# One constant: how many indirect DMAs GpSimd keeps in flight, 3 where it was 2

## The reference: what is computed

```python
xn = layernorm(x)
s  = channel_attention(xn, Wq, Wk, Wv, Wo)        # 256 x 256 scores per sequence, softmax over channels
g  = silu(moe(xn))                                # 32 experts, 8 groups
out = x + s * g

# moe: each row picks 3 of 8 groups by their best score, then 6 experts among those
y = sum over the 6 experts e of weight_e * (silu(xn @ w1[e].T) * (xn @ w3[e].T)) @ w2[e].T
y = y + shared_expert(xn)
```

## Time and profile before

| what | value |
|---|---|
| median of 3 runs | 969.05 us (965.66 to 969.32) |
| the profiled execution, its own time | 964.12 us |
| its span in the trace | 962.4 us |
| TensorE busy | 596.8 us (62%), granted clock 0.804 on average |
| VectorE busy | 506.7 us (53%) |
| GpSimd busy | 399.2 us (41%), 384 indirect DMAs |
| DMA traffic | 174.75 MB, 182 GB/s over the span |

### The profile page before, as it was taken

The page is one execution under the profiler, slowest core; times in us unless marked ns, Lnnn a source line. Parts: engine busy times, 40 slices in busy tenths (PEclk is TensorE's granted clock), DMA queues, the critical chain, the costliest instruction groups (busy, mean ns, idle before and its releaser), DMA issues.

```text
span 962.4 us, 13698 instructions
## 1 busy us (share of the span) xinstructions
PE 596.8 (62%) x3728; PEld 486.4 (51%) x3728; DVE 506.7 (53%) x1412; ACT 341.5 (35%) x684; POOL 399.2 (41%) x401
## 2 busy tenths in 40 slices
PE   5788782928375776001979776758486765658540
PEld 4567551817164654001968665546375654547430
DVE  7877863736374771000535555546465645646543
ACT  3343431332323242001646443435254443435330
POOL 0135345455364663663001444343444444453443
PEclk9798795867768686655979797879799897979875
DMA  9994572634524223224437675758677675848552
GB/s 335 390 356 164 182 262 93 234 132 140 210 73 141 76 93 132 82 82 136 145 120 218 192 237 171 219 154 251 176 220 224 189 208 168 241 148 259 164 170 76
DMA packets 134232, 174.75 MB, mean 182 GB/s; under 512 B 12433, under 2 KB 120722, under 8 KB 133266
## 3 DMA queue, kind: packets, MB, share of 16 engines
q1 hardware_dynamic: 109698, 107.77, 34.3%
q0 software_dynamic: 18432, 50.36, 17.4%
q10 hardware_dynamic: 6032, 15.76, 4.7%
HBM read 81.56 MB, written 92.28 MB: 181 GB/s over the span
## 4 chain that ended last, share of the span: by engine, by line
DMA 57%; issue 21%; POOL 9%; PE 8%; DVE 4%; POOLq 1%; ACT 0%; SPq 0%; DVEq 0%; ACTq 0%
DMA early<-slots_d,slot_at 30%; DMA slots_d<-early,slot_at 23%; POOL slots_d L391 7%; PE ps L696 4%; DMA slots_d<-pad 3%; DVE ps L957 3%; POOL early L408 2%; PE ps L715 2%; PE ps L684 1%; PE ps L706 1%; DVE work L974 1%; POOLq L391 0%; SPq L290 0%; DMA work<-slots_d 0%; DMA slots_d<-early 0%
## 5 line engine op out<-in xcount | busy, mean ns | idle before, releaser
L408 POOL DMA_INDIRECT early<-slots_d,slot_at x192 | 191.7, 999 | 316.9 <-DVE ps L957 108.2
L391 POOL DMA_INDIRECT slots_d<-early,slot_at x192 | 205.4, 1070 | 237.8 <-DMA slots_d<-early,slot_at 170.5
L696 PE MATMUL ps<-w_all,work 128*128 x1344 | 186.5, 294 | 57.3 <-issue 54.2
L696 PEld LDWEIGHTS ps<-w_all,work 128*128 128x128 f16 x1344 | 140.5, 105 | 83.1 <-issue 60.4
L684 PE MATMUL ps<-ident,work 128*128 128x128 f32 x448 | 75.2, 294 | 140.1 <-DMA work<-slots_d 65.9
L957 DVE SCALAR_TENSOR_TENSOR ps<-early,wk,ps 128x256 f32<-128x256 f32 x160 | 77.8, 486 | 116.9 <-DMA early<-slots_d,slot_at 115.5
L684 PEld LDWEIGHTS ps<-ident,work 128*128 128x128 f32 x448 | 54.7, 151 | 155.7 <-issue 81.4
L974 DVE SCALAR_TENSOR_TENSOR work<-ps,work 128x512 f16<-128x512 f32 x112 | 76.8, 686 | 103.6 <-ACT work L517 102.1
L517 ACT ACTIVATE work<-ps 128x512 f16<-128x512 f32 x112 | 66.6, 595 | 141.0 <-PE ps L684 128.1
L715 PE MATMUL ps<-w_all,work 128*128 x672 | 99.9, 289 | 2.5 <-DVE work L987 2.0
L524 ACT ACTIVATE work<-ps 128x256 f32<-128x256 f32 x112 | 43.0, 384 | 157.1 <-PE ps L696 127.4
(11 more groups left out here) (140 smaller groups left out, 811.6 us busy)
## 6 DMA issues: line engine op xcount, KB each, us to landing
work<-slots_d SPq DMA_DIRECT2D x112, 256.0 KB
slots_d<-early SPq DMA_DIRECT2D x112, 256.0 KB
slots_d<-pad SPq DMA_DIRECT2D x7, 3072.0 KB, 15.5
w_all<-in_wexp ACTq DMA_DIRECT2D x7, 1536.0 KB, 6.9
slots_d<-pad SPq DMA_DIRECT2D x1, 7168.0 KB, 30.0
s_all<-in_x SPq DMA_DIRECT2D x8, 512.0 KB, 4.8
ysh_d<-work ACTq DMA_DIRECT2D x8, 512.0 KB
early<-ysh_d SPq DMA_DIRECT2D x32, 128.0 KB
```

What stands on the lines that cost most here:

```text
L391: pool.indirect_dma_start(slots_d[:, :], bass.IndirectOffsetOnAxis(ap=slot_at[:, at:at + 1], axis=0), xn[b % XN_RING][:, t, :], None, boun ...
L408: pool.indirect_dma_start(gath[:, at % RING, :], None, slots_d[:, :], bass.IndirectOffsetOnAxis(ap=slot_at[:, at:at + 1], axis=0), bounds_ ...
L696: mm = pe.matmul(ps[:, 2 + p % 2, h * 2 * I:(h + 1) * 2 * I], xT[p % 2][:, x_low, h, k, :], w16[:, bass.ds(at_weights[2 * p + h] + w_low * ...
```

## The change

The constant is 3 instead of 2:

```diff
 XN_RING = 3
-FLIGHT = 2
+FLIGHT = 3
 BATCH_ROWS = TB * TOP_K
```

## The result

The changed kernel takes 856.75 us (median of 4 runs, 849.25 to 861.13) against 967.99 us before (965.66 to 969.32; also four runs, of which the table ahead of the prediction had three). The ratio is 0.885, with a 95% interval of 0.878 to 0.891. The forecast was 821 us. The profiled execution took 858.25 us, with a span of 856.5 us.

What follows compares the result with a forecast made beforehand. It took the count of indirect DMAs in flight to bound both phases: 962.4 us less 75 (scatters), 57 (gathers) and 12 (tail), plus 1.7 around the span, gives 820.1, named as 821 us; range 785 to 865.

Steps and rivals of the forecast that it cites:

- The count in flight was the limit of both phases: Scatters and gathers: POOL, allowed two in flight, waits for landings; 108.2 us put down to DVE line 957 belong to this.
- full ring: Gathers: the reading, rejected by the prediction, that 108.2 us of POOL's waiting come from all 12 buffers being in use.
- term of 75 us: All 192 scatters: 67 in slow stretches of 166 us, 125 others in 168 us, sum 334, so 75 us saved.
- `normal` stops waiting for scatters: Phase 1, DVE line 755: waits for scatters, such as 16.8 us before `normal(4)`, go or nearly go.
- Twelve pairs take 45.5 us: Phase 2: 12 us around a `hold` plus 34 us at a DMA share of 0.95, about 45.5 us instead of 53.6.
- signs of being wrong: Landings half as long again, POOL's DMA_INDIRECT over 1.0 us, PE waiting for `slots_d`, or similar waits for ring or stores.
- sum for the seven stretches: Phase 2, seven stretches of twelve pairs: 318.5 us instead of 375.4, so 57 us saved.
- The tail: End of phase 2, from 916.50 us with 19 gathers left: end at about 950, 12 us saved, between 8 and 16.
- the gathers gain nothing since the DMA engines are full: Rival, phase 2: the DMA engines bound the gathers, so no gain there; 877 us, 868 with a small gain; chance 0.14.
- both floors are reached: Rival: PE's own pace reached in phase 2, DVE's chain nearly in phase 1; 777 us, 795 with one; chance 0.16.
- It does nothing: Rival: POOL's own issue is already the limit, or the queue works on two at a time; 964 us; chance 0.04.
- slower since loads come late: Rival, phase 2: gathers crowd out loads of pairs (line 330) and PE waits for rows; 971 us; chance 0.02.

Runs made afterwards that it cites:

- e2: Changed kernel with only the gathers at three in flight, the scatters at two as before: 890.57 us, ratio 0.923 to the kernel before.
- e9: The changed kernel without any edit, run again on another chip, the same as for e8: 824.28 us, ratio 0.850 to the kernel before.
- e1: Changed kernel with only the scatters at three in flight, the gathers at two as before: 888.14 us, ratio 0.921 to the kernel before.
- e4: Changed kernel with four in flight for both scatters and gathers instead of three: 771.06 us, ratio 0.796 to 0.803 around 0.799.
- group 2: The runs e5, e6 and e7, made on one chip beside the kernel before: 857.99, 857.35 and 897.99 us, against 969.47 us before.
- e3: Changed kernel, three in flight, with POOL waiting for a small memset of its own after each indirect DMA: 921.56 us, ratio 0.956.
- e7: Changed kernel with six in flight for both scatters and gathers instead of three: 897.99 us, ratio 0.928 to the kernel before.
- e10: The kernel of e4 (four in flight for both) without any edit, on the same chip as e11: 775.72 us, ratio 0.799.
- e11: The kernel of e7 (six in flight for both) without any edit, on another chip: 760.92 us, ratio 0.783 to the kernel before.
- e8: The kernel of e4 (four in flight for both) without any edit, on the same chip as e9: 771.50 us, ratio 0.796.
- e5: The changed kernel itself, run once more without any edit: 857.99 us, ratio 0.882 to the kernel before.
- e6: Changed kernel plus one semaphore that nobody uses, which shifts the numbers of those made after it: 857.35 us, ratio 0.884.

## Why the prediction was right, and where its sizes were off

**The count in flight was the limit of both phases.** Right. The prediction read the 108.2 us that the profile put down to DVE's line 957 as waiting for landings, and e2 shows that the gathers alone, with a third in flight, are worth 73 us. The 71.6 us that the profile puts down to this line after the change are again no full ring, and only in part landings. I took the last 180 gathers and, for each wait over 0.4 us, the latest of its conditions. Before, all 145 such waits (215 us) end with a landing. In e9 66 do (78 us), and 8 others, of 50 us, end with the landing of a pair's **store**, up to 7.5 us each, one for each `hold` after which PE's pairs come late. In the result it is 68 us for landings and 89 for stores, if a store lands 3.2 us after its issue as in the earlier trace rows. With four in flight it is 23 us for landings and 81 for stores, with six 0.5 and 98. So a limit that bound no gather before is the next one. The prediction had it only among its signs of being wrong. Gather 60 of e9, where the profile again names DVE, and the store it needed; that store landed at 572.36, while the sum that frees the buffer had ended 10.9 us before the gather's start:

```profile
564.81 0.99 POOL L408 DMA_INDIRECT early<-slots_d,slot_at  x1 [0.30 <-issue]
573.25 0.99 POOL L408 DMA_INDIRECT early<-slots_d,slot_at  x1 [7.45 <-DVE ps L957]
...
568.53 0.36 SPq L334 DMA_DIRECT2D slots_d<-early  x1
```

**A scatter costs 1.28 us in quiet, and three go in a slow landing's time.** Right, as the rows of POOL above show. Counted as in the prediction (a landing over 3 us makes a slow place), the result has 65 scatters in slow stretches of 165.5 us, forecast 67 in 166. The other 127 take 1.43 us each, forecast 1.34. So of the term of 75 us, e9 has 68.4 and e1 73.4 us. That a third is worth nothing in quiet is refuted by e1's gain and the spacing of 1.28 for 1.59 us. The 3.17 us of the prediction have two parts. In e2's quiet scatters, two in flight as before, the last of the 16 landing increments comes 2.41 us after the issue starts, and the scatter that waits for it starts 0.76 us later. The 2.3 us that the prediction estimated by the Trainium skill (DMA: Bandwidth & Descriptors, section "Anatomy of one DMA — SWDGE (gpsimd) path") agree with the 2.41. What the conclusion drawn from them left out is the 0.76 us that POOL needs to start again. In the result itself it was 62.1 us, and the missing part is the late increments: DVE's `slot_at` of sequences 2 to 6 came 38.4 to 40.0 us apart, instead of the 37.6 of a chain that doesn't wait, and that of sequence 7 after 81.8 us, at 341.6, where e9 has it at 306.1.

**`normal` stops waiting for scatters.** Nearly. The wait of 16.8 us before `normal(4)` is gone, line 755 follows line 748 at once:

```profile
146.33 0.16 DVE L748 TENSOR_TENSOR rstd<-rough,newt 128x4 f32<-128x4 f32 x1
146.56 1.38 DVE L755 TENSOR_SCALAR early<-s_all,mv,rstd 128x256 f32<-128x256 f32 x4
```

In e9 two such waits are left, of 15.5 us together. The last scatter was forecast at 370; it is issued at 382.95 after, at 376.65 in e9.

**Twelve pairs take 45.5 us.** Right in e9 (317.2 / 7 = 45.3) and e2 (45.2), 49.4 in the result. Its working was less good than its outcome, and that the two agree is in part luck: it took the DMA engines as the limit, at a share of 0.95 outside the `hold`, and forecast a share above 0.8. The share is 0.78 to 0.79. Its sum slips too: 12 + 34 is 46 us, which is 53 us saved and not 57. With four and six in flight the same stretches fall only to 43.0 and 43.4 us at 0.81, as this window of e4 shows:

```profile
436.10:737.40 301.30, 243.36 (x2019) 210.48 (x2017) 209.24 (x475) 156.60 (x364) 166.29 (x166) 0.90 0.81 253
```

So three in flight still cost 2 us per 12 pairs in the count itself. With four and six, most of what the gathers still wait is for stores (above); what sets the 43 us was not taken apart. That a third gather lengthens the others' landings could be seen to be small: the mean from a gather's issue to the end of its last packet is 3.24 us before, 3.43 after and 3.53 in e9.

**The step that was mis-sized.** It is the sum for the seven stretches, with 57 us forecast and 29.5 measured in the result. The prediction let every wait of ACT and DVE for PE last as long as before. In e9, where they did, the term is 58.2 us (375.4 to 317.2). In the result 45 evictions started late by 65.6 us. The stage table splits the 33.3 us by which the result's span exceeds e9's, for one and the same program: 6.3 us up to the first load, 28.8 in the seven stretches, 0.3 between, and 2.1 the other way in the tail. No step of the prediction had a place for this, and the trace before gave no cause to look: 4 late starts of 448.

**The tail.** Forecast 12, measured 14.2 and 12.1. The last gather starts 8.7 us before the end, as before.

**The rivals.** That the gathers gain nothing since the DMA engines are full fell with e2. That both floors are reached fell too: with three in flight neither was, and with six some 38 us per sequence, against 37.6 for DVE's own chain, and 43.4 us per 12 pairs, against 41.8, came near. "It does nothing" and "slower since loads come late" did not occur. There was one rival missing, on the slow side: that PE's increments come late while POOL issues without a pause. It took 33 us here, and didn't change the sign. The range held the result (856.75 against 865), but its upper part had been made for gathers that gain little, which is not what happened: that it held is luck.

**What stays open.** Why increments of PE arrive late in the result and in group 2, and not in the three other groups, is not settled. In the runs that have it, most late starts stand where POOL issues without a pause; in the runs that don't, such issuing does nothing. Whether it is the chip or what went on on it at the time, these runs can't tell; each chip was met once, and the result's own is not known. Nor can they tell whether the delay would be there without the profiler's recording, whose records are incomplete just where it occurs. Whether four in flight would suffer, and whether the pause of e3 would protect, was not measured where it occurs. Since the pause costs some 100 us (921.56 for e3, 824.28 for e9), it would not be worth it there either: even e7, at 898, is faster than e3.

**The best version** is four or six in flight. Six is best where nothing comes late (760.9 us, ratio 0.783) and worse than three where it does (898 against 858). Four gave 771 to 776 us on three chips, but wasn't run where something comes late, so which number is safer is open. From four to six, e10 to e11 on one chip, it is 14.8 us: the first load moves from 346.7 to 333.6, and the stretches hardly gain (from the first matmul of line 696 for pair 24 to that for pair 108: 305.5 in e10, 304.1 in e11).

## What to carry to other kernels

Where an engine issues small DMAs one after the other, compare the time from issue to release with the time of an issue. Their quotient says how many must be in flight, and it has to be taken under load: here 3.2 / 1.3 in quiet but 6.6 / 1.3 beside other traffic, and going from three to four still gave 32 us of the first phase (first load at 379.3 in e9, 347.2 in e8, one chip). Then look for the next condition behind the one removed; here it was the stores. Run a change on more than one chip, and where a "remote" wait stands on a single core compare the waiting instruction's start with the end of what it waits for: the same program differed by 4.1% between chips, and by 18% with six in flight, while the kernel before differed by 0.7%.

## What the runs showed of the hardware

- PE's semaphore increments reached DVE and ACT up to 41 us late (45 us in e5) while POOL issued indirect DMAs every 1.28 us, and the last of them were seen 6 us after the last scatter's issue began. In phase 2 evictions that wait for them started up to 4.5 us late. ACT's and DVE's increments were not late. Four traces showed it (the result, e5, e6, e7), and those of nine runs on three chips did not, two of them with the very programs of e5 and e7. The cause is open.
- A quiet scatter of 128 rows of 1 KB, from the start of its issue (e2): the first DMA packet starts at 1.54 us, the last ends at 2.06, the last landing increment comes at 2.41, and a scatter that waits for it starts at 3.17.
- POOL issues such a scatter every 1.28 us (0.97 busy, 0.30 between) for as long as nothing holds it, a gather every 1.30. A one-element memset that is waited for makes that 1.86 us.
- More indirect DMAs in flight hardly lengthen each other: a gather takes 3.24 us from issue to the end of its last packet with two in flight, 3.53 with three (e9), 3.53 with four (e4) and 3.66 with six (e11), as means over 192.
